# A two-layer transformer kernel whose experts' rows go through in 39 tiles of 256 places in place of 23 tiles of 512

## What is computed

```python
gates = xf @ gate_w.T + gate_b                      # 4096 rows, 8 experts
weights, indices = jax.lax.top_k(gates, 2)
weights = softmax(weights, axis=-1)
for e in range(8):
    w_e = sum(weights * (indices == e), axis=-1, keepdims=True)
    h = gelu(xf @ w1[e] + b1[e])                    # 128 -> 512
    out = out + w_e * (h @ w2[e] + b2[e])           # 512 -> 128
```

## Time and profile before

| | |
|---|---|
| median of three runs | 824.44 us (820.56 to 825.52) |
| the profiled execution | 825.4 us, span of its instructions 823.7 us |
| busy time in the span | PE 676.8 (82%), DVE 564.8 (69%), ACT 416.2 (51%), POOL 262.6 (32%) |
| expert stage, first product of tile 0 to last result stored | 166.2 to 323.7 us |
| moved in the whole span | HBM read 47.38 MB, written 23.08 MB |

### The profile page before, as it was taken

How to read it: one execution, slowest core, us unless ns; L and a number is a source line. 1 busy time by engine, 2 the same in 40 slices (tenths; PEclk the granted TensorE clock), 3 DMA queues, 4 the chain that set the end, 5 groups by cost and what they waited for, 6 DMA issues and landing times.

```text
span 823.7 us, 9538 instructions
## 1 busy us (share of the span) xinstructions
PE 676.8 (82%) x3009; PEld 486.1 (59%) x3009; DVE 564.8 (69%) x1389; ACT 416.2 (51%) x701; POOL 262.6 (32%) x215
## 2 busy tenths in 40 slices
PE   3697542089999999059998999989999989999897
PEld 1586531068787888035546855557755568555575
DVE  4776768166676774657787678787587876784663
ACT  2556333067776763214527644357545276442573
POOL 3316767500000001726720237512077202242000
PEclk8778755589999998559999999999999999999999
DMA  5305566756766771100000000000010000000000
GB/s 200 129 1 189 190 242 262 262 159 230 239 240 229 259 248 58 45 0 21 22 10 2 1 35 23 20 1 1 13 33 21 12 1 1 25 2 1 0 1 27
DMA packets 22458, 71.09 MB, mean 86 GB/s; under 512 B 4924, under 2 KB 6212, under 8 KB 18120
## 3 DMA queue, kind: packets, MB, share of 16 engines
q1 hardware_dynamic: 18312, 62.08, 21.5%
q0 software_dynamic: 4096, 8.40, 3.1%
HBM read 47.38 MB, written 23.08 MB: 86 GB/s over the span
## 4 chain that ended last, share of the span: by engine, by line
PE 58%; DVE 17%; POOL 10%; issue 6%; ACT 4%; DMA 3%; SPq 0%; DVEq 0%; ACTq 0%; POOLq 0%
PE ps L1424 15%; PE ps L1420 9%; PE ps L1426 8%; PE ps L1658 7%; PE ps L1428 6%; PE ps L1427 6%; POOL rows_by_expert L505 6%; PE ps L1646 2%; DVE stats L904 2%; PE ps L1674 2%; POOL yb L521 2%; DMA wbuf<-w_split 2%; DVE ring L1317 1%; DVE cmat L1380 1%; DVE yb L1220 1%
## 5 line engine op out<-in xcount | busy, mean ns | idle before, releaser
L521 POOL DMA_INDIRECT yb<-y_by_expert,ypos x64 | 62.1, 970 | 181.2 <-DMA y_by_expert<-ysb 165.2
L1424 PE MATMUL ps<-hid,fh 128*128 128x512 f32 x256 | 103.4, 404 | 5.1 <-DVE hid L1301 5.1
L1426 PE MATMUL ps<-hid,fh 128*128 128x512 f32 x256 | 100.8, 394 | 0.0
L505 POOL DMA_INDIRECT rows_by_expert<-h,pos x64 | 68.0, 1062 | 35.6 <-issue 18.4
L561 POOL TENSOR_TENSOR misc<-misc,ring 128x1024 f32<-128x1024 f32 x28 | 65.9, 2355 | 38.9 <-DVE ring L1291 31.2
L1301 DVE TENSOR_TENSOR hid<-ring,hid 128x512 fp32r<-128x512 f32 x56 | 38.5, 688 | 41.1 <-ACT hid L790 39.5
L1195 DVE TENSOR_TENSOR hid<-ring,hid 128x512 fp32r<-128x512 f32 x46 | 31.8, 692 | 42.9 <-ACT hid L592 42.9
L1424 PEld LDWEIGHTS ps<-hid,fh 128*128 128x128 f32 x256 | 48.2, 188 | 21.0 <-DVE hid L1301 10.4
L1658 PE MATMUL ps<-ring,hn 128*128 128x512 f32 x112 | 55.6, 618 | 5.3 <-DVE ring L1291 5.3
L1674 PE MATMUL ps<-attnT,cmat 128*128 128x512 f32 x128 | 56.9, 592 | 0.0
L1426 PEld LDWEIGHTS ps<-hid,fh 128*128 128x128 f32 x256 | 48.2, 188 | 10.1
(11 more groups left out here) (282 smaller groups left out, 1702.5 us busy)
## 6 DMA issues: line engine op xcount, KB each, us to landing
wbuf<-w_split SPq DMA_DIRECT2D x23, 1024.0 KB, 5.3
w_split<-parts SPq DMA_DIRECT2D x4, 2048.0 KB, 7.8
xs<-rows_by_expert SPq DMA_DIRECT2D x23, 256.0 KB, 5.3
y_by_expert<-ysb SPq DMA_DIRECT2D x23, 256.0 KB, 5.6
raw<-in_w SPq DMA_DIRECT2D x8, 512.0 KB, 9.0
ffn_raw<-in_ffn SPq DMA_DIRECT2D x1, 2816.0 KB, 14.8
rows_by_expert<-zeros SPq DMA_DIRECT2D x9, 256.0 KB, 2.0
xa<-in_x SPq DMA_DIRECT2D x4, 512.0 KB, 6.3
```

The lines of the kernel that those rows point to most:

```text
L505: gp.indirect_dma_start(disp, bass.IndirectOffsetOnAxis(pos[:, b, k, t:t + 1].bitcast(U32), 0), h1[:, b % 2, t, :], None).then_inc(scatter ...
L521: gp.indirect_dma_start(yb[:, k, t, :], None, ydisp, bass.IndirectOffsetOnAxis(ypos[:, b, k, t:t + 1].bitcast(U32), 0))\
L1424: te.matmul(out_, w(0), x(0), start=first, stop=False)
L1426: return te.matmul(out_, w(0), x(1), start=False, stop=last_)
```

## The change

The tiles are 256 places wide (`HW = GW // 2`). `width(j)` gives `HW` for each, since the number of wide tiles `WIDE` is 0; there are `(8192 + 8 * 255) // 256` = 39 of them. Every instruction of a tile has half the elements, the rows and results move 128 KB in place of 256 KB, and there are two transposes in place of four each way. The weights of the expert, 1 MB, are loaded for each of the 39 tiles. The order of the loops, the three slots of `wbuf` and `xs`, and the list of SyncE are as before; the loops have 39 rounds in place of 23.

The plan is written so that it could hold wide and half tiles at once: it works on 16 segments (8 wide, 8 half) in place of 8. With `WIDE` = 0 the wide part stays, as instructions, and its results put no tile there.

```diff
+HW = GW // 2
+WIDE, HALVES = 0, (B * N * TOP_K + E * (HW - 1)) // HW
-NT = (B * N * TOP_K + E * (GW - 1)) // GW
+NT = WIDE + HALVES
+
+TILE_ORDER = list(range(NT))
...
+        def width(j):
+            return GW if TILE_ORDER[j] < WIDE else HW
...
             def weights(j):
-                sp.reg_load(which, expert[0:1, j:j + 1])
+                sp.reg_load(which, expert[0:1, TILE_ORDER[j]:TILE_ORDER[j] + 1])
                 load(f(wbuf[:, j % 3]).rearrange("p w s n -> p (w s n)"),
                      wsplit[bass.ds(sp.snap(which), 1)].rearrange("o p n -> p (o n)"), m_w[j % 3])
 
             def tile_rows(j):
-                sp.reg_load(row, xbase[0:1, j:j + 1])
-                load(xs[:, j % 3], disp[bass.ds(sp.snap(row), GW), :].rearrange("(p i) d -> p i d", i=GT), m_x[j % 3])
+                n = width(j) // 128
+                sp.reg_load(row, xbase[0:1, TILE_ORDER[j]:TILE_ORDER[j] + 1])
+                load(xs[:, j % 3, 0:n], disp[bass.ds(sp.snap(row), n * 128), :].rearrange("(p i) d -> p i d", i=n),
+                     m_x[j % 3])
...
             def first_product(j):
                 pe.wait_ge(*loaded(m_w, j))
                 pe.wait_ge(*md_lo.done(j))
+                n = width(j)
                 for c in cs:
                     if j:
                         pe.wait_ge(*ma_gelu.done((j - 1, c)))
-                    three(ps[:, 2 + c, :], lambda i: wbuf[:, j % 3, 0, i, c * 128:(c + 1) * 128], lambda i: hT[:, j % 2, i, :],
-                          True, True).then_inc(*mp_f.raise_((j, c)))
+                    three(ps[:, 2 + c, 0:n], lambda i: wbuf[:, j % 3, 0, i, c * 128:(c + 1) * 128],
+                          lambda i: hT[:, j % 2, i, 0:n], True, True).then_inc(*mp_f.raise_((j, c)))
```

More of the change, by code:

```diff
@@ L710, in gelu @@
                     act.wait_ge(*md_split.done((j - 1, c)))
-                bias = b1sel[:, j, c:c + 1]
+                n, bias = width(j), b1sel[:, TILE_ORDER[j], c:c + 1]
                 if c in ACT_HI:
@@ L1027, in positions @@
                 v.tensor_copy(pos[:, b], posf[:, b]).then_inc(*dve_pos.raise_(b))
+            SIZE, START, SHIFT, WIDE_AT, HALF_AT, PAST = 0, 1, 2, 3, 4, 5
+            wide, half = slice(0, E), slice(E, 2 * E)
             def plan_tiles():
@@ new lines, in plan_tiles @@
+                settle(own, v.tensor_reduce(size, mcmp[:, :, 0:E], X, ALU.add))
+                settle(own, v.tensor_tensor(size[:, half], size[:, half], size[:, wide], ALU.subtract))
+                settle(own, v.tensor_tensor(mcmp[:, :, :], size.unsqueeze(1).broadcast_to([128, 2 * E, 2 * E]),
+                                            upto[:, :, :], ALU.mult))
+                ends, past = mseg[:, 6, :], mseg[:, PAST, 0:1]
+                settle(own, v.tensor_reduce(ends, mcmp[:, :, :], X, ALU.add))
@@ new lines, in plan_tiles @@
+                settle(own, v.tensor_tensor(start, ends, size, ALU.subtract))
+                v.tensor_copy(shift[:, wide], start[:, wide])
+                settle(own, v.tensor_tensor(shift[:, half], start[:, half], size[:, wide], ALU.subtract))
+                settle(own, v.scalar_tensor_tensor(shift.rearrange("p (a e) -> p a e", a=2),
+                                                   shift.rearrange("p (a e) -> p a e", a=2), -float(GW),
+                                                   erow[:, :].unsqueeze(1).broadcast_to([128, 2, E]), ALU.mult, ALU.add))
@@ L1058, in plan_tiles @@
+                v.tensor_copy(xbase[:, :], mten[:, 5, :])
+                v.tensor_copy(expert[:, :], mten[:, 3, :])
+                settle(own, v.tensor_tensor(ended_at[:, :, 0:E], ended[:, :, wide], ended[:, :, half], ALU.add))
+                mine = ended_at[:, :, 0:E]
+                settle(own, v.tensor_tensor(mpick[:, :, :, :], mine.unsqueeze(2).broadcast_to([128, NT, HC, E]),
                                             b1[:, :].rearrange("p (e c) -> p c e", e=E).unsqueeze(1)
@@ new lines, in y_positions @@
+                past, n = mseg[:, PAST, 0:1], B * TOP_K * T
+                begin, step, from_, halves = mseg[:, WIDE_AT, wide], mseg[:, WIDE_AT, half], mseg[:, HALF_AT, wide], mseg[:, HALF_AT, half]
+                settle(own, v.scalar_tensor_tensor(from_, size[:, wide], float(GW), erow[:, :], ALU.mult, ALU.add))
+                settle(own, v.tensor_scalar(begin, start[:, half], past, float(WIDE), ALU.add, ALU.add))
+                settle(own, v.scalar_tensor_tensor(halves, start[:, half], 2.0, begin, ALU.mult, ALU.min))
@@ L1581, in x_transposed @@
                     pe.wait_ge(*md_lo.done(j - 1))
-                transposes(0, [xs[:, j % 3, i, :] for i in range(GT)]).then_inc(*mp_x.raise_(j))
+                transposes(0, [xs[:, j % 3, i, :] for i in range(width(j) // 128)]).then_inc(*mp_x.raise_(j))
             def first_product(j):
@@ L1605, in y_transposed @@
                     pe.wait_ge(*md_y.done(j - 1))
-                transposes(1, quarters(yT[:, j % 2, :])).then_inc(*mp_y.raise_(j))
+                transposes(1, quarters(yT[:, j % 2, :])[0:width(j) // 128]).then_inc(*mp_y.raise_(j))
             x_transposed(0)
```

140 lines of the change are left out of this document (79 added, 61 removed).

## The result

The kernel before took 824.77 us (median of six, 820.56 to 825.6), the changed one 872.37 us (median of six, 869.96 to 880.64). The ratio is 1.061, with a 95% interval of 1.057 to 1.065: slower by 6%, within the range and 5 us from the forecast of 867. The profiled execution of the changed kernel is the longest of its six (880.64 us, span 878.3), so its trace shows some 8 us more than the median has; its own account comes first, and how it stands to the median afterwards.

What follows compares the result with a forecast made beforehand. TensorE was taken to bound the kernel, only just, with weight loads nearly as long as a round. Stage +31, start +2 and clock +10 gave +43 us on the profiled 825.4, about 867 us by the median; range 848 to 892.

Steps and rivals of the forecast that it cites:

- L = 6.0: Expert stage: time from a round's end to the matmul using the newly loaded weights, 0.47 issue, 5.45 landing, 0.05 wake-up, unchanged.
- w = 3.5: Expert stage: a narrow round's work in us, TensorE about 3.4 with matmuls at 0.122, against a round of 6.35 before.
- The bound of 0.19: Upper bound in us for a 256-wide matmul on TensorE, if the weight load no longer hides behind it; 0.122 was taken.
- Rounds in pairs, 9.5 us: Expert stage: two rounds run back to back, then TensorE stands 2.5 us; 4.75 a round, stage +31 us.
- faster: Rival: loads land so early that only work counts, stage about 15 us sooner, 810 us; chance 0.03.
- no change: Rival: within 1% (8 us), 826 us, stage equal to before at a landing of 3.7 us; chance 0.06.
- The counted parts: Sum for the expert stage: 13.0 to round 3, 166.3 for 35 steps, 3.5, 1.7 and 4.1 at the end: 188.6 us.
- The clock (+10): TensorE waits in the expert stage lose full clock in four of 18 pairs, some 2.4 us each: +10 us.
- the cold rival: Rival: TensorE loses the clock in nearly every pair, or narrow matmuls do not halve; all pairs cold 900 us; chance 0.28.
- The start (+2): Start of the expert stage: longer plan delays three weight loads, rows of tile 0 queue behind them; +2 us (0 to 4).
- The estimate from figures of the Trainium skill: Expert stage by the skill's pages: w 3.05 to 3.5, L 4.9, stage about 12 us longer in place of 31.
- The transfers (3.85 us a round at 340 GB/s): Expert stage: weights stay 1 MB a round, rows fall to twice 128 KB; 1.31 MB take 3.85 us, below 4.75 a round.

Runs made afterwards that it cites:

- half-load run of the kernel before: Kernel before the change (23 tiles of 512), only the first matrix of an expert (512 KB) loaded from tile 3 on: 833.38 us against 835.76, ratio 0.998.
- split loads: Changed kernel, each tile's weights in two 512 KB transfers with a semaphore each, the first asked for when first_product has read it: 830.42 us, ratio 1.008.

## Why the prediction was right, point by point

**Landing and slot (L = 6.0): right.** Issue 0.47 us after the end of the round (197.96 back to the last matmul's end at 197.49), landing 5.33 in the mean, 0.05 for the wake-up: 5.85. The load of 1 MB did not land sooner with smaller rows behind it, as was said.

**Work of a round (w = 3.5): right.** 3.46 without loads, 0.12 us from matmul to matmul. The bound of 0.19 was not needed.

**Rounds in pairs, 9.5 us: right.** Pairs at full clock measure 3.47 + 5.8 = 9.3; "faster" and "no change", which needed landings of 3.3 and 3.7 us, fell with the first row. The counted parts: from the first product of tile 0 to round 3 14.4 us (I had 13.0), the tail from round 38 on 11.0 (9.3). Both have a clock in them that these terms left out: it was granted at half from 168.8 to 176.4 us, over the first rounds (before the change too, up to 170.0), and fell again at 367.5, in round 38. The DMA share, about 0.8 by the prediction, was 0.69.

**The clock (+10): the right sign, built from two wrong numbers.** I had four cold pairs at 2.4 us. There were 14 falls, and most cost 1.2 to 1.5 (4.94 - 3.47 = 1.47). The step that failed is the price, "a round at half clock costs 6.0 in place of 3.5", put on every cold pair. A round that is cold throughout does cost that: the one from 334.52 to 340.46 took 5.94. But it was the only one; elsewhere the clock came back inside the round (0.65 in the mean, and matmuls 0.12 apart at its end). The count failed because I judged by one waiting stretch from each side; here TensorE stood for 2.0 to 2.5 us in one piece, once 3.4, which is what the new order does to every pair. From round 3 on the 35 steps took 184.6 us. At 9.3 a pair they would take 162.8. Of the other 22, 18 are the clock: 13 of the falls lie in these steps, twelve make their rounds longer by 18.2 us together, and one is hidden, since its round waits for the load of 7.37 anyway. The rest is the late loads (7.37 and 6.79 in the chain). The 14th fall is in the tail, which makes about 20 us for the clock in the stage.

*The profiled execution and the median.* The mean granted clock of the profiled execution was 0.874, in the other five it lay between 0.878 and 0.895, 0.891 in the one of 872.98 us. One fall lowers a round of 4.94 us to a mean of 0.65, a deficit of 0.35 x 4.94 = 1.7; the difference of 0.017 over 873 us is a deficit of 15, so as an estimate 8 or 9 falls fewer, 13 us at 1.47 each; the difference of the two times is 7.7, which is five. By this the median has some five to nine falls and 8 to 13 us for the clock, near the +10 of the sum; in the profiled execution the term is 20. That the sum met the median at 5 us is partly luck: too few falls, each too dear. No other execution was traced, so the count in the median is not shown.

The Trainium skill (TensorE: Matmul & The Clock Gate, section HAM oscillation) describes a loop that waits for its loads and runs cold in each step, as the cold rival had it. The trace agrees in the count and not in the price: the clock fell in 14 of 18 pairs, but most falls took 1.2 to 1.5 us out of 10.7, and not the 2.4 of that rival.

**The start (+2): right in size, wrong in its way.** The first product of tile 0 started at 168.8, 2.6 us later. I had said that the rows of tile 0 would stand behind the three loads of weights. They did not: they landed in 1.98 us (2.38 before). It was the last scatter, which they wait for, that landed late: issued at 159.29 in place of 158.32 and landed in 5.10 us in place of 2.21. From the chain of the kernel before:

```profile
158.32 2.21 DMA rows_by_expert<-h,pos
```

The run that moved two of the loads shows that they are the cause of the landing (2.24 again). Rows behind loads that are still under way do land late, as the prediction has it, when the weights are issued late: in 7.76 us in the half-load run of the kernel before. Here the last of the three loads had landed at 164.34, and the rows were asked for at 164.94. The plan took 7.0 us more (the zeros were issued from 145.80 in place of 138.79) against 7 to 8 in the sum, the weights 7.4 later, and neither stood in the chain.

**The estimate from figures of the Trainium skill: read too narrowly.** A stage "about 12 us longer" comes near with w = 3.5 alone (168.2 us, 10.7 more); with its w of 3.05 the same sum gives 159.0 us, 1.5 more than before, which could not have been told from no change. The 4.4 us come from a fit that the Trainium skill (DMA: Bandwidth & Descriptors, section Anatomy of one DMA) heads as the path of GpSimd, while these loads go through SyncE's hardware queue. Measured are w = 3.46 and L = 5.85.

**The transfers (3.85 us a round at 340 GB/s): right, and it only binds once the latency is gone.** With split loads it sets the rounds at 3.92.

## What to carry to other kernels

When tiles are made smaller and each brings a load of fixed size, compare the round not with the transfer's bytes over the bandwidth but with its time from request to landing, divided over the rounds that lie between the freeing of a slot and its use. Here the share of the DMA engines stood at 0.7 while loads set the pace, and the cure was an earlier request for the part of the slot that is free first, at the same bytes. Where rounds of two lengths can be had, a load per tile costs least on the long ones: with split loads 12 wide and 15 narrow tiles beat both 23 wide and 39 narrow. With whole loads they did not (1.011, 0.999 to 1.023). 23 wide tiles with split loads were not run; there the loads are covered but for the two waits, 2 us in all.

## What the runs showed of the hardware that was not expected

- A load of half the bytes is not twice as fast: in the changed kernel 1 MB landed in 5.3 us and 512 KB in 4.0 in the mean. From these two, as an estimate, 1.3 us go with 512 KB (some 400 GB/s) and 2.7 us do not go with the bytes. In the kernel before, with larger transfers of rows behind each load, the same halving took the mean from 5.45 to 4.31 us. In the changed kernel the next load was mostly asked for 3.3 us after the first, while that was still under way, so none of these is the landing of a load by itself.
- Of 18 waits of 2.0 to 3.4 us in one piece 14 came with a fall of the clock, in rounds that kept TensorE busy for 0.77 of the time. The narrow rounds with half loads (0.85 busy, waits of up to 1.2 us, in most rounds and not in every second one) kept full speed for the whole stage. In the run with the eight more matmuls waits of up to 1.6 us left the clock at full speed and the one of 2.27 came with its only fall.
- Small transfers with large ones under way: the scatter of rows landed in 5.10 us with three loads of 1 MB under way and in 2.2 without, though it goes through another queue. Single scatters on GpSimd took 1.90 us in place of 0.95 between 152 and 156 us, while the zeros and these loads were being issued; before the change such ones stand at 141.4 (3.02) and 144.8 (1.90), with the zeros, but one of 2.02 in the changed kernel, at 141.5, stands ahead of them. What lengthens them is not shown.
- The same SyncE instructions for eight transfers took 6.42 us in one execution and 13.85 in another on another chip. What slowed them is not shown.
